# Splitting four more weight pairs per chunk in a recommendation tower, with a reordered start

## The reference, cut to what matters

```python
e = jnp.stack([tbl_0[ids[:, 0]], ..., tbl_31[ids[:, 31]]], axis=1)     # 512 x 32 x 16
x0 = h = e
for i in range(3):
    z = (x0[:, :, None, :] * h[:, None, :, :]).reshape(B, F * G, E)
    y = relu(einsum('oc,bce->boe', Ws[i], z) + bs[i][None, :, None])   # 128 channels out
    x_keep, h = (y[:, :64, :], y[:, 64:, :]) if i != 2 else (y, y)
    xs.append(x_keep)
h = concatenate([sum(concatenate(xs, axis=1), axis=2), dense_ctx], axis=1)
h = maximum(h @ W_top1 + b_top1, 0.0)
h = maximum(h @ W_top2 + b_top2, 0.0)
y = h @ W_top3
```

## Time and profile before

| what | us |
|---|---|
| median of three runs | 572.45 |
| the profiled execution, its own time | 572.41 |
| its span (first to last instruction) | 570.4 |
| outside the span | 2.0 |
| PE busy | 526.1 |
| DVE busy | 359.9 |
| POOL busy | 191.6 |
| ACT busy | 135.6 |
| one steady turn | 30.42 |
| PE's first record (the transposes) | at 10.57 |
| DVE's first product of (1,0,0) | at 29.75 |
| PE's last record of layer 1, chunk 0 | ends at 48.7 |
| turn c = 3 starts on PE | at 145.83 |

### The profile page before, as it was taken

One profiled execution on the slowest core, in us unless ns is written; L12 is line 12 of the kernel. 1 busy time (PEld: TensorE's weight loads), 2 busy tenths in 40 slices (PEclk: granted clock), 3 DMA queues, 4 the chain that ended last, 5 costly groups with the idle time before them and its releaser, 6 DMA issues.

```text
span 570.4 us, 3875 instructions
## 1 busy us (share of the span) xinstructions
PE 526.1 (92%) x1362; PEld 255.9 (45%) x1362; DVE 359.9 (63%) x212; ACT 135.6 (24%) x193; POOL 191.6 (34%) x162
## 2 busy tenths in 40 slices
PE   2986079699999999999999999999999999999998
PEld 2632034345454544445454545454544445454445
DVE  1243157393949586776949393939495876857642
ACT  1111014312314041414131222213040414130313
POOL 5770072635160707061524334251703030300000
PEclk9988769989999999999999999999999999999999
DMA  6799898279697969697969797796968595540100
GB/s 220 144 187 212 194 263 177 57 201 200 154 230 155 224 146 226 143 230 151 229 141 227 152 239 162 188 214 148 225 149 228 135 236 132 131 94 9 71 0 1
DMA packets 33588, 94.46 MB, mean 166 GB/s; under 512 B 7889, under 2 KB 15057, under 8 KB 25122
## 3 DMA queue, kind: packets, MB, share of 16 engines
q1 hardware_dynamic: 26402, 91.47, 67.3%
q0 software_dynamic: 4096, 1.06, 1.6%
q10 hardware_dynamic: 3072, 1.70, 1.4%
HBM read 92.04 MB, written 2.10 MB: 165 GB/s over the span
## 4 chain that ended last, share of the span: by engine, by line
PE 84%; DMA 8%; POOL 3%; DVE 2%; ACT 1%; issue 1%; ACTq 1%; SPq 0%; DVEq 0%
PE acc L559 74%; PE acc L570 7%; DMA x_rot<-x_scratch 4%; POOL gathered L313 3%; DMA x_scratch<-gathered 2%; DMA gathered<-in_table,rows_all 2%; PE acc L580 1%; DVE z L378 1%; PE acc L575 1%; ACT h L472 0%; DMA row<-in_row 0%; DVE z L366 0%; ACTq L259 0%; PE h L580 0%; ACT kept L472 0%
## 5 line engine op out<-in xcount | busy, mean ns | idle before, releaser
L559 PE MATMUL acc<-z,w_direct 128*128 128x512 f32 x1024 | 451.3, 601 | 31.2 <-DVE z L378 25.7
L559 PEld LDWEIGHTS acc<-z,w_direct 128*128 128x128 f32 x1024 | 196.5, 193 | 276.6 <-issue 243.3
L378 DVE TENSOR_TENSOR z<-h,x_pair 128x2048 f32<-128x2048 f32 (+1 forms) x65 | 144.9, 2250 | 141.3 <-ACT h L472 135.2
L326 POOL TENSOR_TENSOR z_low<-z,z_high 128x1024 fp32r<-128x1024 f32 x30 | 70.2, 2361 | 260.8 <-ACT z_high L458 260.8
L313 POOL DMA_INDIRECT gathered<-in_table,rows_all x128 | 121.1, 946 | 40.7 <-issue 36.0
L378 DVE TENSOR_TENSOR z<-h_odd,x_pair 128x2048 f32<-128x2048 f32 x32 | 72.2, 2279 | 8.8 <-ACT h_odd L472 8.8
L378 DVE TENSOR_TENSOR z<-h_even,x_pair 128x2048 f32<-128x2048 f32 x32 | 72.2, 2279 | 5.2 <-ACT h_even L472 5.2
L472 ACT ACTIVATE h<-acc,columns 64x512 f32<-64x512 f32 x32 | 20.8, 652 | 221.0 <-PE acc L570 215.5
L458 ACT ACTIVATE z_high<-z 128x1024 fp32r<-128x1024 f32 x30 | 30.1, 1049 | 72.4 <-DVE z L366 72.4
L472 ACT ACTIVATE kept<-acc,columns 64x512 f32<-64x512 f32 (+1 forms) x48 | 32.8, 683 | 54.6 <-PE acc L559 53.8
L366 DVE TENSOR_TENSOR z<-x_rep,x_rot 128x2048 f32<-128x2048 f32 x15 | 34.2, 2280 | 16.6 <-DMA x_rot<-x_scratch 16.6
(11 more groups left out here) (119 smaller groups left out, 116.4 us busy)
## 6 DMA issues: line engine op xcount, KB each, us to landing
x_pair<-x_scratch SPq DMA_DIRECT2D x128, 512.0 KB, 6.8
x_rot<-x_scratch SPq DMA_DIRECT2D x56, 256.0 KB, 5.2
x_rep<-x_scratch SPq DMA_DIRECT2D x14, 256.0 KB, 5.0
w_direct<-in_W SPq DMA_DIRECT2D x2, 1024.0 KB, 8.9
gathered<-in_table,rows_all POOLq DMA_INDIRECT x128, 7.1
x_scratch<-gathered SPq DMA_DIRECT2D x30, 64.0 KB, 9.3
x_rot<-x_scratch ACTq DMA_DIRECT2D x4, 256.0 KB, 18.2
x_pair<-in_W_top SPq DMA_DIRECT2D x2, 512.0 KB, 4.3
```

The source lines that it names most:

```text
L326: nc.gpsimd.tensor_tensor(z_low[:, slot_of(pair)], products_of(pair), z_high[:, slot_of(pair)].bitcast(F32), ALU.subtract).then_inc(low_po ...
L378: nc.vector.tensor_tensor(z[:, step.group % Z_SLOTS, first:end], h[:].unsqueeze(1).to_broadcast([P, end - first, N]), x_pair[:, chunk % 2, ...
L559: op = nc.tensor.matmul(acc[pair.layer][:], w_direct[:, first + i], products_of(pair)[:, i], start=i == 0 and pair is OPENS[pair.layer, pa ...
```

## The change

Four pairs of layers 1 and 2 are now split as layer 0's are: (1,k=0,i=1), (1,k=1,i=1), (2,k=1,i=1) and (2,k=2,i=1), for chunks 1 to 15. Their weights are rounded and split once, at the start. Every split pair is used two steps later. `z_high` and `z_low` have four slots instead of three; to make room, the perceptron's split weights share memory with `z_high`, `z_low`, `w_high` and `w_low`. Layers 1 and 2 get two PSUM banks each, used by turns, and the points at which ACT writes outputs are set by a table. POOL issues one gather behind each of eight steps in place of eight in a row. At the start, the first chunk's `x_pair` halves go to two queues (SP and ACT), the store and `load_x0` of chunk 1 move to SP ahead of chunk 1's `x_pair`, `turn_dense` moves ahead of the transposes, of which 56 are left, and in `FIRST` step (0,2,0) comes directly behind (1,1,0).

```diff
-Z_SLOTS, PAIR_SLOTS, X_SLOTS = 5, 3, 4
+Z_SLOTS, PAIR_SLOTS, X_SLOTS = 5, 4, 4
-BUSY = 64
+BUSY = 56
...
-         + [(1, 1, 0), (1, 1, 1), (0, 2, 0), (1, 1, 2), (1, 1, 3)])
+         + [(1, 1, 0), (0, 2, 0)] + [(1, 1, k) for k in range(1, GROUPS)])
+SPLIT = ((1, 0, 1), (1, 1, 1), (2, 1, 1), (2, 2, 1))
+AT = {(0, 0, 0): 0, (0, 0, 1): 2} | {of: GROUP + 2 * n for n, of in enumerate(SPLIT)}
...
+def hands(layer, chunk, k):
+    return tuple("pool" if chunk and (layer, k, i) in AT else "tensor" for i in range(2))
...
+    at = {(0, c): PLACE[1, c, 0] for c in range(CHUNKS)}
+    at |= {(1, c): PLACE[2, c - 1, GROUPS - 1] if c >= 2 else PLACE[2, c, 0] for c in range(CHUNKS)}
+    at |= {(2, c): PLACE[2, c + 1, 0] if c else PLACE[1, 1, 1] for c in range(CHUNKS - 1)}
...
-            due[n + (2 if pair.layer == 0 else 1)].append(pair)
+            due[min(n + 2, len(PLAN) - 1)].append(pair)
...
+        banks = [[acc[0], acc[0]], [spare, acc[1]], [x_bank, acc[2]]]
...
+        def load_half(eng, c, k, a):
+            rows = x_dram[c, ROT * a + GROUP * k:ROT * a + GROUP * (k + 1), :]
+            eng.dma_start(x_pair[HALF * a:HALF * (a + 1), c % 2, GROUP * k:GROUP * (k + 1), :],
+                          rows.unsqueeze(0).to_broadcast([HALF, GROUP, N])).then_inc(xp_here[c % 2][k], 16)
...
             store_x(sp, 0)
-            for c in range(2):
-                for k in range(GROUPS):
-                    load_pair(c, k)
+            sp.wait_ge(x_stored[0], 32)
+            for k in range(GROUPS):
+                load_half(sp, 0, k, 0)
+            store_x(sp, 1)
+            sp.wait_ge(start_done, 1)
+            load_x0(sp, 1)
+            for k in range(GROUPS):
+                load_pair(1, k)
...
-                    for j in range(GATHERS):
-                        gather(ahead, j)
+                for c in range(AHEAD, CHUNKS):
+                    j = n - PLACE[1, c - AHEAD, 0]
+                    if 0 <= j < GATHERS:
+                        if j == 0 and c >= X_SLOTS:
+                            before = c - X_SLOTS
+                            pool.wait_ge(x_stored[before % 2], 32 * (before // 2 + 1))
+                            if before == 0:
+                                pool.wait_ge(first_here, 16)
+                        gather(c, j)
...
+            act.wait_ge(dense_turned, 1)
+            nc.scalar.activation(dense_high[:], dense_bank[0:COPIES * EMBED, :], ACT.Copy).then_inc(dense_rounded, 1)
+            act.wait_ge(x_stored[0], 32)
+            for k in range(GROUPS):
+                load_half(act, 0, k, 1)
...
-                if pair is OPENS[pair.layer, pair.chunk] and pair.chunk:
-                    pe.wait_ge(kept_out[pair.layer], pair.chunk)
+                used = pair.chunk if pair.layer == 0 else pair.chunk - 1
+                if pair is OPENS[pair.layer, pair.chunk] and used > 0:
+                    pe.wait_ge(kept_out[pair.layer], used)
...
             pe.wait_ge(w_ready, 2)
+            turn_dense()
             for _ in range(BUSY):
```

More of the change, by code:

```diff
@@ L80, in step @@
         pairs = []
-        for i, by in enumerate(hands(layer, chunk)):
+        for i, by in enumerate(hands(layer, chunk, k)):
             pairs.append(Pair(layer, chunk, k, i, counts["group"], by, counts[by], counts["split"]))
@@ L116 @@
 CLOSES = {(pair.layer, pair.chunk): pair for pair in ORDER}
-assert not BEHIND[len(PLAN)] and not BEHIND[len(PLAN) + 1]
+LAST1 = max((pair for step in PLAN for pair in step.by("pool") if step.layer < 2), key=lambda pair: pair.split)
+LAST_SLOT = max((pair for step in PLAN for pair in step.by("pool") if pair.split % PAIR_SLOTS == PAIR_SLOTS - 1),
+                key=lambda pair: pair.split)
+assert LAST_SLOT.chunk < CHUNKS - 1 and AT[SPLIT[1]] + 2 == 2 * N // P and SPLIT[1][0] == 1
 def flat(tiles):
@@ L195, in dlrm_tower @@
         wd = x_pair[0:COPIES * EMBED, 0, 10, :]
+        wt1_high, wt1_low = z_high[:, PAIR_SLOTS - 1], z_low[:, PAIR_SLOTS - 1]
+        wt2_high, wt2_low = [flat(w[:, 0:2 * N // P]) for w in (w_high, w_low)]
         sum01_high, sum01_low = zl_high[:], zl_parts[:]
@@ L565, in split @@
                 open_bank(pair)
-                slot = slot_of(pair)
+                slot, at = slot_of(pair), AT[pair.layer, pair.k, pair.i]
+                if pair.split == 0:
+                    pe.wait_ge(w_ready, 2 + len(SPLIT))
                 pe.wait_ge(low_dve if pair.by == "vector" else low_pool, pair.count + 1)
```

106 lines of the change are left out of this document (51 added, 55 removed).

## The result

The changed kernel takes **548.69 us** (median of 4 runs, 548.26 to 549.1) where the kernel before takes 571.92 beside it: ratio 0.9596, 95% interval 0.9577 to 0.9615. The forecast was 530.4 us, 525 to 544: the direction was right, the size was not, and the time lies outside the range.

The account below looks back on a forecast made before the run. PE's own work bounds the kernel from turn c = 3 on, a wait ahead of that. Gains of 22.2 (start), 19.0 (split pairs) and 0.8 us (tail) sum to 42.0: span 528.4, plus 2.0 outside it, 530.4 us; range 525 to 544.

Parts of the forecast that it names:

- the new work stays hidden because the engines' sums fit: Steady turns: POOL's 24.2, ACT's 7.8 and DVE's 21.7 us all stay below PE's 29.0 us.
- the rate of 350 GB/s: Start: two queues feeding both SBUF halves load chunk 0's `x_pair` at 350 GB/s, 4.19 MB in 12 us.
- the walk of turn c = 2: Start: PE followed step by step, idling 3.3 us plus 1.9 for the clock; turn c = 3 starts at 123.6, not 145.8.
- The saving of a pair: Layers 1 and 2: a split pair takes 1.371 us against 1.717 direct, saving 0.346; a steady turn becomes 29.04 us.
- the PSUM bank: Layers 1 and 2: a second bank removes the 4.64 us wait at the start and 0.78 us at the tail.
- the loss by `turn_dense`: Start: waiting for the dense rows ahead of PE's transposes costs 2.2 us.
- Part 1: Split pairs of layers 1 and 2: 55 pairs behind the start of turn c = 3 save 19.0 us.
- Rival B: Behind layer 0's block: the 1.35 us slack is missing, each turn loses 1.38 us, 548 us; chance 0.11.
- Rival C: Turns: POOL decides if subtractions exceed 3.4 us; standing still for a DVE product each gives 646 us; chance 0.03.
- Part 2: The start: faster loads and earlier stores bring turn c = 3 forward, a gain of 22.2 us.
- Rival A: Start: two queues bring nothing, chunk 2's `x_rot` is ready at 79.3 instead of 71, 538.2 us; chance 0.27.
- Part 3: The tail: the second bank removes 0.78 us; making the perceptron's split weights late costs nothing.

Follow-up runs that it names:

- a run in which every `x_pair` load is fast: Changed kernel with each `x_pair` transfer carrying two rows to all 128 partitions, wrong fields in the upper half: 542.75 us, ratio 0.9476 to the kernel before.
- the early load alone: Changed kernel with chunk 2's store and `load_x0` moved ahead of chunk 1's later `x_pair` loads on SP: 543.9 us, ratio 0.9486 to the kernel before.

## Why the forecast was wrong

Three steps of the prediction failed: that the new work stays hidden because the engines' sums fit, the rate of 350 GB/s, and the sizes in the walk of turn c = 2. The saving of a pair, the PSUM bank and the loss by `turn_dense` held.

**Part 1, the saving of a pair: right but for small change.** A turn is 29.13 us where 29.04 was forecast: a split block of six records takes 1.39 us, not 1.371. DVE's wait for `h1` fell to 6.66 us (7.3 forecast). Rival B (slack behind the layer-0 block) did not come. The count was off: 17.3 us of pairs lie behind the start of turn c = 3, not 19.0.

**Part 1, POOL's 24.2 of 29.0 us, "so no engine's sum reaches PE's": the overlap that failed.** Sums of busy time say nothing on which instruction stands beside which. I had named the rule (the Trainium skill, "SBUF — State Buffer", "Who interferes with whom") and set it aside, since subtractions took 2.37 us with DVE busy beside them. That row showed DVE products with one input in PSUM. The instructions of the rule were two on DVE's list, and the trace agrees with it for them: they grew from 2.28 to 3.03 us and from 0.74 to 2.86, and the subtractions beside them too (4.43 and 2.82 us in turn 13). In ten turns this hides; in turns 13 and 14 it costs 3.8 us, at the start 1.9 once the load is in time, at the tail, with the weights' split, about 1.6. Rival C had the mechanism, but priced it as if every subtraction stood still and POOL were the limit, and so got 3%; what became late was DVE's next `z`.

**Part 2, 350 GB/s: the largest miss.** Two queues to the two halves gave 224 to 246, one queue 211 and 220. Rival A said so, and so did the Trainium skill's same page ("Can I just issue two DMAs to hit both halves?"), which has two concurrent transfers at only 6% more than one; here it is 2 to 17%. The price did not come where I had put the data first: layer 1 of chunk 0 ended at 48.7 us, 48.9 forecast, with the slow rate too. It came through chunk 1's store, through at 41.9 in place of 34.8, and the loads behind it: chunk 2's `x_rot` landed at 80.5 us (71 forecast, 79.3 by A) and DVE waited 7.8 us for it (7.2 by A). The measured price of the rate is 5.8 us, in a run in which every `x_pair` load is fast, chunk 1's too; the early load alone gave 5.1. The forecast took the value near the 128-partition rows, though what the change does is two transfers to 64 partitions each, and the nearest rows for that were the 214 ones.

**Part 2, the walk of turn c = 2: mis-sized by 4.3 us** even with all data there. I had a wait of 3.3 us and 1.9 for the clock. Measured with the fast loads: 5.17 (1.9 more, `square_parts`), about 2.7 for the clock behind it (0.8 more), and 1.8 behind the second gap of 2.14 us, where I had 0.5 (8 records in 5.40 us, against 3.60 elsewhere). That is 4.0 of the 4.3; the rest I cannot place. The granted clock there, in the changed kernel:

```profile
105.80:109.00 3.20, 3.17 (x4) 1.31 (x5) 3.20 (x3) 0.99 (x1) 2.51 (x3) 0.55 0.11 13
```

Most of it stands at the lower of the two levels, 1.2 GHz, behind a wait of 2.1 us. 5.8 and 4.3 are the 10.1 us of the start. The walk had the pair that is missing ahead of the wait, but not that the split pairs' subtractions also hold up `square_parts` there.

**Part 3** was right on the bank and missed POOL: the last two subtractions took 8.01 us where two take 4.74, beside the split of the perceptron's weights, and PE waited 1.55 us.

**The rivals.** A was right in what it said of the rate and gave 538.2, short by 10.5 us: the long turns, the walk, the count and the tail came on top. Each was small, and all had the same sign, so a range that took in one rival at a time did not hold the sum.

## What to carry to other kernels

Before adding work to an idle engine, list what each neighbour does at that moment, not how busy it is: here DVE's instructions with two SBUF inputs and POOL's subtractions shut each other out, and what a queue puts ahead of an instruction (eight gathers, 11 us) can cost more than the work saved. A saving per instruction counts only where its engine is the bound; where PE waits for DVE, deferring its work makes the wait longer. And a repair may be added work: two turns of unused gathers made this kernel faster.
